# A fused transformer kernel on one core: position bias of the first attention as narrow tile matmuls, one spread matmul issued earlier, and matmuls added beside a bitwise search

## The chip, the cores and the metric

The kernel is one program for one core of a Trainium2 chip. The metric is the device time of one execution in microseconds (us), lower is better. The cores' engines are called by their short names: PE is TensorE (PEld its weight loads), DVE VectorE, ACT ScalarE, POOL GpSimd, SP SyncE, which here only issues DMAs.

## The reference

Eight residual layers run over x of 32 batches x 256 tokens x 128 channels. Three of them matter here.

```python
# layer 1: attention, 16 heads of 8 channels, bias by distance
x = x + _L0_attn_ref(_layernorm(x), Wq, bq, Wk, bk, Wv, bv, rel_bias)
#   scores = einsum('bqhd,bkhd->bhqk', q, k) / sqrt(8) + rel_bias[bucket(k - q)]
#   out = softmax(scores) @ v
# layer 4: experts that choose tokens
#   scores = softmax(xt @ Wr);  G, idx = top_k(scores.T, k)   # k = 2048 of 8192 tokens, 8 experts
# layer 5: state space
#   h = exp(dt*A) * h + (dt*u) * B;  y = sum_n h[n] * C[n]    # 16 states, 256 channels
```

The bucket of the bias depends on n = max(q - k, 0) alone: bucket n for n < 16, then up to bucket 31, which is reached at n near 31 and kept from there on. So the bias of a head is one constant (bucket 31) for keys far behind the query, another (bucket 0) for keys after it, and it varies only in a strip of some 31 keys.

## The kernel before

The eight layers run one after the other, each in a block of its own in which every engine has its own instruction stream, in the order of the Python code; semaphores tie the streams together. Nothing reorders the work but that written order.

**First attention** (`attention` with `causal` false, some 630 us). Work is per batch b (32 of them) in a software pipeline of eight slots j, two heads per slot. In a slot TensorE makes for two heads

- `maxima` (L623, L630): the scores with queries on the partitions, for each half t of the queries, 2 matmuls of 256 columns from 96 contraction rows, plus the bias of the strip from `bmax` through a reversing permutation `flip` (256 columns for t = 0, 320 for t = 1). VectorE reduces them to row maxima (L574).
- `scores_near` (L640): the scores again with keys on the partitions, first 128 keys, 2 matmuls of 256 columns from 128 rows. Their bias is not added by TensorE but by VectorE, `add_band` (L524), on the scores in PSUM; ScalarE takes exp of the sum (L413).
- `scores_far` (L652, L659): the other 128 keys, with the bias by three matmuls of 256 columns (`bexp`, the float32 bias in three bf16 parts). ScalarE takes exp (L416).
- every other slot `values` (L671, L675): probabilities times V for four heads, whose outputs stand on 32 partitions each, so each matmul uses 32 columns of the array at one of four positions. `turn` (L682) transposes them.

The constant part of the bias comes through six contraction rows (`CROW`), three for each half of the keys. The tables of the bias are made at the start by `BiasSetup`: a look-up matmul, a copy, a split into three bf16 parts, a store to DRAM, and loads into `bmax`, `bexp` and, by matmuls (L753) and copies (L562), `band`.

**The search** (`choose`): a 30-step bitwise search for the k-th largest score. Each step counts on VectorE (L1616), sums over partitions by a matmul with one column (L1592) and takes a decision on VectorE (L1619 to L1627).

**The state space layer** (`state_space`): for each group of 512 tokens and each state n of 16, POOL makes the input (L2208), ACT exp (L2369), DVE the scan (L2486) and the product with C (L2498, or POOL for the states in `MOVED` = (2, 5)), PE adds the product up (L2613). C reaches DVE through PSUM: `spread_C` (L2581) writes `CC`, one buffer. `front` puts the next group's projections between them.

Of the kernel before, what the change touches and what calls it, by code (L numbers as in the profile page):

```python
# [146 lines left out]
def attention(nc, res, name, w, causal, held):  # L147
# [5 lines left out]
    BAND = 160  # L153
    FIRST = 8
    K0Q, K1Q = S, (P if causal else S)
    with ExitStack() as ctx:
# [18 lines left out]
        FROM = S - BAND  # L175
# [18 lines left out]
        else:  # L194
            bmax = sc.sb("bmax", [P, H, BAND], BF16)
            bexp = sc.sb("bexp", [P, NPART, H, BAND], BF16)
            flip = sc.sb("flip", [P, P], BF16)
            band = sc.sb("band", [P, H, BAND])
# [6 lines left out]
                "o_ev ot_mm cseq fin rseq yt_mm yt_ev pr_mm pr_done band_mm band_ev biased bsplit bplaced "  # L205
# [3 lines left out]
        BANDS = [range(h, min(h + 3, H)) for h in range(0, H, 3)]  # L209
# [14 lines left out]
        else:  # L224
            loads = [(wqkv[:], w["wqkv"]), (bqk[:], w["bqk"]), (bv[:], w["bv"]), (flip[:], w["flip"])]
# [3 lines left out]
            bias = BiasSetup(nc, sc, w, bmax, bexp, BAND, [Sx[0], Sx[1], SA[0]], probs)  # L229
# [5 lines left out]
        with nc.Block() as block:  # L235

            @block.sync
            def _(sp):
# [4 lines left out]
                def constants(k, sem):  # L243
                    sp.wait_ge(s["k_cleared"], k + 1)
                    sp.dma_start(Kp[k][MROW:MROW + 2], w["krows"][0:2]).then_inc(sem, 16)
                    sp.dma_start(Kp[k][CROW:CROW + 6], w["krows"][2:8]).then_inc(sem, 16)
                    sp.wait_ge(s["cleared"], k + 1)
                    sp.wait_ge(bias.crows_stored, NPART * 16)
                    sp.dma_start(Qp[k][CROW:CROW + 6], bias.crows).then_inc(sem, 16)

                if causal:
                    for k in range(BUF):
                        sp.dma_start(Qp[k][CROW:CROW + 6], w["zrows"]).then_inc(s["consts"], 16)
# [9 lines left out]
                def step(b, k, a, x_, m, c, p):  # L263
                    if a:
                        kb = (k + 3) % BUF
                        dram = packing[kb % 2]

# [3 lines left out]
                        if causal and b == -1:  # L271
                            sp.wait_ge(s["bsplit"], 5)
                            for i in range(NPART):
# [5 lines left out]
                                     parts[:, 1, 0:2, :]).then_inc(s["written"], 16)  # L279
                        wait(sp, s["written"], 32 * (b + 4))  # L280
# [8 lines left out]
                    if not causal and b == -3:  # L289
                        bias.store(sp)  # L290
                        constants(0, s["consts"])
                        constants(1, s["consts"])
# [65 lines left out]
            def _(act):  # L358
# [48 lines left out]
                def step(b, k, a, x_, m, c, p):  # L407
                    for j in range(8):
                        if c:
                            at = 2 * j % NP  # L410
                            wait(act, s["pv_done"], 16 * b + 2 * j + 2 - NP)
                            wait(act, s["sa_mm"] if causal else s["biased"], 8 * b + j + 1)
                            nc.scalar.activation(probs[:, at:at + 2, 0:K0Q], pair(SA[j % 2], K0Q), ACT.Exp)\  # L413
                                .then_inc(s["ea_done"], 1)
                            wait(act, s["sb_mm"], 8 * b + j + 1)
# [22 lines left out]
                    if not causal and b == -2:  # L438
# [3 lines left out]
                        bias.place(act)  # L442
# [4 lines left out]
            def _(v):  # L447
# [2331 lines left out]
```

## Time and profile before

| | |
|---|---|
| median of 3 runs | 3942.99 us (3940.44 to 3944.78) |
| the profiled execution: own time, span | 3959.12 us, 3956.8 us |
| busy share of the span | PE 86%, DVE 73%, ACT 48%, POOL 39% |
| first attention | from about 44 us to 696 us |
| the search | 1514 to 1573 us |
| state space layer | about 2060 to 3040 us |

A share over the whole span mixes layers with different limits, so each layer is read for itself. A matmul's record shows its latency, not the time for which it holds the array: that is read from the distance between the starts of successive matmuls. A float32 matmul leaves two records.

### The profile page before, as it was taken

The numbers are of one execution on the slowest core, as the hardware profiler recorded it, in microseconds if no ns is written. First come the engines' busy times: TensorE is split into PE (matmuls) and PEld (weight loads), VectorE is DVE, ScalarE is ACT, GpSimd is POOL, SyncE is SP. The second block draws the span as 40 slices with busy tenths as digits, with TensorE's granted clock in tenths as the row PEclk, the third lists the DMA queues.
The fourth block names the chain that finished last, engine by engine and source line by source line (L and its number), as shares of the span: only waits on it lengthen the run. The fifth ranks groups of instructions, "written<-read, shape, count | busy, mean of one in ns | idle before, by whom it ended". The sixth has DMA issues, their size and how long they took to land. (4 is left out here: it accounts for less than half of the span.)

```text
span 3956.8 us, 60602 instructions
## 1 busy us (share of the span) xinstructions
PE 3403.3 (86%) x20989; PEld 2093.9 (53%) x21044; DVE 2900.9 (73%) x6458; ACT 1902.9 (48%) x3463; POOL 1549.3 (39%) x1015
## 2 busy tenths in 40 slices
PE   5999999878999984677748888888886999999987
PEld 3677776555777762344423333333333666666653
DVE  7888888556777756433239999999997777777765
ACT  2555556324665651222237676776673333333325
POOL 2311111542211200588848877878873011111112
PEclk9999999999999996799869999999998999999998
DMA  6333332004444424233332332322321222222211
GB/s 154 94 89 90 88 89 54 1 5 115 100 101 104 98 62 122 57 44 44 43 78 73 95 100 83 93 78 73 95 79 60 90 87 87 87 87 87 88 59 43
DMA packets 242530, 314.19 MB, mean 79 GB/s; under 512 B 46450, under 2 KB 157779, under 8 KB 231588
## 3 DMA queue, kind: packets, MB, share of 16 engines
q1 hardware_dynamic: 208308, 289.02, 26.3%
q0 software_dynamic: 22528, 17.32, 3.3%
q10 hardware_dynamic: 11392, 3.97, 0.5%
q8 instruction: 172, 2.82, 0.3%
q14 instruction: 130, 1.06, 0.1%
HBM read 251.93 MB, written 57.08 MB: 78 GB/s over the span
## 5 line engine op out<-in xcount | busy, mean ns | idle before, releaser
L574 DVE TENSOR_REDUCE a_Mx<-a_Sx 128x2 f32<-128x512 f32 (+1 forms) x1024 | 590.3, 618 | 172.2 <-PE a_Sx L626 126.7
L2208 POOL TENSOR_TENSOR a_inp<-a_dtu,a_Bs 128x1024 f32<-128x1024 f32 x256 | 597.8, 2359 | 67.9 <-DMA a_Bs<-a_brows 42.5
L2486 DVE TENSOR_TENSOR_SCAN a_h<-a_dA,a_inp 128x1024 f32<-128x1024 f32 x256 | 583.0, 2283 | 31.7 <-ACT a_dA L2369 27.2
L2613 PE MATMUL a_Y<-a_hc,g_ident 128*128 128x512 f32 x1024 | 487.8, 599 | 7.4 <-POOL a_hc L2222 3.5
L347 POOL TENSOR_TENSOR a_rest<-a_qk,a_parts 128x512 f32<-128x512 f32 x64 | 75.2, 1175 | 916.1 <-ACT a_parts L399 916.1
L413 ACT ACTIVATE a_Pr<-a_SA 128x512 f32<-128x512 f32 x512 | 305.4, 596 | 168.6 <-DVE a_SA L524 79.6
L623 PE MATMUL a_Sx<-att_Kp,att_Qp 96*128 96x256 bf16 (+1 forms) x2048 | 345.3, 261 | 42.7 <-DMA att_Qp<-a_crows 17.9
L2369 ACT ACTIVATE a_dA<-a_dtA,a_A 128x512 f32<-128x512 f32 x512 | 329.8, 681 | 97.5 <-DVE a_h L2486 96.5
L1958 ACT ACTIVATE f_sg<-f_GB 128x512 f32<-128x512 f32 x272 | 162.6, 598 | 436.6 <-PE f_GB L2034 436.4
L2084 PEld LDWEIGHTS f_OUT<-g_routed_wd,f_hm 128*128 128x128 f32 x2176 | 280.6, 191 | 123.5 <-issue 90.5
L2613 PEld LDWEIGHTS a_Y<-a_hc,g_ident 128*128 128x128 f32 x1024 | 195.4, 194 | 234.2 <-issue 223.0
L2498 DVE TENSOR_TENSOR a_hc<-a_h,a_CC 128x1024 f32<-128x1024 f32 x224 | 273.5, 1221 | 43.0 <-DMA f3e_xg<-f_rows,f3e_idx 14.4
L1900 DVE TENSOR_TENSOR f_sg<-f_sg,f_UB 128x512 f32<-128x512 f32 x256 | 175.4, 685 | 168.6 <-PE f_UB L2036 114.7
L2084 PE MATMUL f_OUT<-g_routed_wd,f_hm 128*128 128x128 f32 x2176 | 289.6, 276 | 3.0 <-DVE f_hm L1904 1.4
L416 ACT ACTIVATE a_Pr<-a_SB 128x512 f32<-128x512 f32 (+1 forms) x512 | 253.1, 494 | 60.2 <-PE a_SB L659 37.0
L2034 PE MATMUL f_GB<-f_xnT,g_routed_wg 128*128 128x512 f32 x544 | 280.8, 598 | 0.0
L2036 PE MATMUL f_UB<-f_xnT,g_routed_wu 128*128 128x512 f32 x544 | 278.7, 594 | 0.0
L623 PEld LDWEIGHTS a_Sx<-att_Kp,att_Qp 96*128 96x128 bf16 x2048 | 189.7, 99 | 80.0 <-DVE a_Mx L574 25.8
L1284 POOL DMA_INDIRECT f_sum<-f3e_Y,f3e_idx x128 | 202.7, 1584 | 56.3 <-issue 41.8
L1273 POOL DMA_INDIRECT f3e_xg<-f_rows,f3e_idx x128 | 124.8, 975 | 224.3 <-DVE f3e_idx L1343 185.6
L1904 DVE TENSOR_TENSOR f_hm<-f_sg,f_Cs 128x512 f32<-128x512 f32 x256 | 189.9, 742 | 10.4 <-DMA f_Cs<-f_crows 1.7
L640 PE MATMUL a_SA<-att_Qp,att_Kp 128*128 128x256 bf16 x1024 | 190.2, 274 | 3.0 <-ACT a_Pr L413 0.6
(480 smaller groups left out, 6771.3 us busy)
## 6 DMA issues: line engine op xcount, KB each, us to landing
a_Bs<-a_brows SPq DMA_DIRECT2D x256, 256.0 KB, 3.3
f_Cs<-f_crows SPq DMA_DIRECT2D x512, 128.0 KB, 2.9
att_Qp<-a_packing SPq DMA_DIRECT2D x192, 192.0 KB
att_Kp<-a_packing SPq DMA_DIRECT2D x192, 192.0 KB
a_packing<-a_parts SPq DMA_DIRECT2D x64, 384.0 KB
a_packing<-a_parts SPq DMA_DIRECT2D x64, 128.0 KB
a_Cs<-a_brows SPq DMA_DIRECT2D x32, 256.0 KB, 4.7
g_x<-x SPq DMA_DIRECT2D x8, 512.0 KB, 7.3
```

The costliest lines, as they stand in the source:

```text
L413: nc.scalar.activation(probs[:, at:at + 2, 0:K0Q], pair(SA[j % 2], K0Q), ACT.Exp)\
L416: nc.scalar.activation(probs[:, at:at + 2, K0Q:K0Q + K1Q], pair(SB, K1Q), ACT.Exp)\
L574: nc.vector.tensor_reduce(Mx[(k + 2 - (j < LATE)) % 2][:, t, 2 * jj:2 * jj + 2], Sx[t][:, 0:2 * wd].rearrange("p (h q) -> p h q", h=2), AX ...
L623: nc.tensor.matmul(both[:, u], Qp[kb][0:KM, h, t * P:t * P + P], Kp[kb][0:KM, h, 0:wd], start=(u == 0), stop=False)
L2034: nc.tensor.matmul(GB[k][:], wg[:, q], xnT[j][:], start=True, stop=True).then_inc(s["g_mm"], 1)
L2036: nc.tensor.matmul(UB[k][:], wu[:, q], xnT[j][:], start=True, stop=True).then_inc(s["u_mm"], 1)
L2084: last = nc.tensor.matmul(OUT[j][:, t], hm[k][:, t * P:t * P + P], wd[:, q], start=False, stop=(q == NQ - 1 and t == G - 1))
L2208: nc.gpsimd.tensor_tensor(inp[n % Q][:], dtu[k][:], Bs[n % Q][:].unsqueeze(1).to_broadcast([P, CH, GT]), ALU.mult).then_inc(s["mulB"], 1)
L2369: nc.scalar.activation(dA[m % 2][:, c], dtA[k][:, c], ACT.Exp, scale=A[:, c, n:n + 1])\
L2486: nc.vector.tensor_tensor_scan(h[n % 2][:].rearrange("p c q -> p (c q)"), dA[m % 2][:].rearrange("p c q -> p (c q)"), inp[n % Q][:].rearra ...
L2498: nc.vector.tensor_tensor(hc[n % Q][:], h[n % 2][:], CC[:].unsqueeze(1).to_broadcast([P, CH, GT]), ALU.mult).then_inc(s["mulC"], 1)
L2613: nc.tensor.matmul(Y[c][:], ident[:], hc[n % Q][:, c], start=False, stop=(n == N - 1))\
```

## The change

Three edits. In the first attention the constant part of the bias becomes a step per 32 keys: 24 contraction rows (8 steps x 3 bf16 parts) in place of 6, and the rest, which is not zero only near the diagonal, is added by blocks of 32 rows x 64 columns. One block matmul has 96 contraction rows (the three parts stacked) and 32 outputs, and four of them stand at the four column positions of the array. `maxima`, `scores_near` and `scores_far` each get such a group of four in place of their former bias; `add_band`, `band`, `bmax`, `bexp` and `flip` go. In the state space layer `spread_C` for states 3 and 6 is issued one place earlier, ahead of the sum of states 1 and 4. In the search four matmuls of 512 columns whose result nobody reads follow each one-column matmul.

```diff
@@ maxima
-                            lo, hi = (0, P) if t == 0 else (FROM, S)
-                            last = nc.tensor.matmul(both[:, :, lo:hi], flip[:],
-                                                    bmax[:, 2 * j:2 * j + 2, P * (1 - t) + lo - FROM:P * (1 - t) + hi - FROM],
-                                                    start=False, stop=True)
-                        last.then_inc(s["mx_mm"], 1)
+                            for r in range(4):
+                                q0 = t * P + 32 * r
+                                lo = max(q0 - 32, 0)
+                                last = nc.tensor.matmul(both[32 * r:32 * r + 32, :, lo:q0 + 32], fold[:],
+                                                        near_q[:, 2 * j:2 * j + 2, lo - q0 + 32:64],
+                                                        start=False, stop=True)
+                                last.then_inc(s["mx_mm"], 1)
+                def add_bias(both, h0, first_key, done):
+                    for r in (3, 0, 1, 2):
+                        q0 = first_key + 32 * r
+                        hi = min(q0 + 64, S)
+                        nc.tensor.matmul(both[32 * r:32 * r + 32, :, q0:hi], fold[:], near_k[:, h0:h0 + 2, 0:hi - q0],
+                                         start=False, stop=True).then_inc(done, 1)
@@ scores_near
+                        add_bias(both, h0, 0, s["sa_mm"])
@@ scores_far
-                        for i in range(NPART):
-                            last = nc.tensor.matmul(both[:, :, P:2 * P], flip[:], bexp[:, i, h0:h0 + 2, 0:P],
-                                                    start=False, stop=(i == NPART - 1))
+                        add_bias(both, h0, P, s["sb_mm"])
@@ vector
-                def add_band(b, j):
-                    v.wait_ge(s["sa_mm"], 8 * b + j + 1)
-                    near = pair(SA[j % 2], K0Q)[:, :, 0:BAND]
-                    nc.vector.tensor_tensor(near, near, band[:, 2 * j:2 * j + 2], ALU.add).then_inc(s["biased"], 1)
@@ scalar
-                            wait(act, s["sa_mm"] if causal else s["biased"], 8 * b + j + 1)
+                            wait(act, s["sa_mm"], W * (8 * b + j + 1))
@@ tensor, before the maxima of batch 1
-                            pe.wait_ge(bias.band_placed, NPART * 16)
-                            for g, hs in enumerate(BANDS):
-                                wait(pe, s["band_ev"], g - 1)
-                                for i in range(NPART):
-                                    last = nc.tensor.matmul(
@@ BiasSetup.place, now on the SP queue
-        eng.dma_start(self.bmax[:], bass.AP(self.lines.tensor, N + S - self.BAND,
-                                            [[1, P], [3 * N, H], [1, self.BAND]])).then_inc(self.placed, 16)
-        for i in range(self.NPART):
-            eng.dma_start(self.bexp[:, i], bass.AP(self.lines.tensor, i * H * 3 * N + S - P,
-                                                   [[1, P], [3 * N, H], [1, self.BAND]])).then_inc(self.band_placed, 16)
+        for dst, at, placed in ((self.near_q, 96, self.placed_q), (self.near_k, 0, self.placed_k)):
+            for i in range(self.NPART):
+                eng.dma_start(dst[32 * i:32 * i + 32], bass.AP(self.lines.tensor, i * H * N + at,
+                                                               [[1, 32], [N, H], [1, 64]])).then_inc(placed, 16)
@@ choose, tensor
                 nc.tensor.matmul(CT[:, 0:1], same[:], cnt[:], start=True, stop=True).then_inc(total, 1)
+                for i in range(BESIDE if b < BITS else 0):
+                    nc.tensor.matmul(IDLE[:], identb[:], identb[:].unsqueeze(1).to_broadcast([P, BL, P]),
+                                     start=True, stop=True)
@@ state_space, tensor
-                    if on(0) and n < N - 1 and n + 1 not in MOVED:
+                    if on(0) and n < N - 1 and n not in MOVED and n + 1 not in MOVED:
                         spread_C(g * N + (n + 1), n + 1, k)
@@
                         wait_product(pe, g * N + n)
+                        if n + 1 in MOVED:
+                            spread_C(g * N + (n + 2), n + 2, k)
```

On TensorE a slot of the first attention (one with `values`) reads so before:

```order
L640 MATMUL a_SA<-att_Qp,att_Kp 128x256 x2
L652 MATMUL a_SB<-att_Qp,att_Kp 128x256 x2
L659 MATMUL a_SB<-a_bexp,a_flip 128x2x128 x3
L623 MATMUL a_Sx<-att_Kp,att_Qp 128x256 x2
L630 MATMUL a_Sx<-a_bmax,a_flip 128x2x128
L623 MATMUL a_Sx<-att_Kp,att_Qp 128x256 x2
L630 MATMUL a_Sx<-a_bmax,a_flip 128x2x160
L671 MATMUL a_O<-a_Pr,att_V 32x256 x4
L675 MATMUL a_O<-a_Pr,att_V 32x256 x4
```

And the same slot of the changed kernel:

```order
L635 MATMUL a_SA<-att_Qp,att_Kp 128x256 x2
L627 MATMUL a_SA<-a_near_k,a_fold 32x2x64 x4
L649 MATMUL a_SB<-att_Qp,att_Kp 128x256 x2
L627 MATMUL a_SB<-a_near_k,a_fold 32x2x32
L627 MATMUL a_SB<-a_near_k,a_fold 32x2x64 x3
L606 MATMUL a_Sx<-att_Kp,att_Qp 128x256 x2
L615 MATMUL a_Sx<-a_near_q,a_fold 32x2x32
L615 MATMUL a_Sx<-a_near_q,a_fold 32x2x64 x3
L606 MATMUL a_Sx<-att_Kp,att_Qp 128x256 x2
L615 MATMUL a_Sx<-a_near_q,a_fold 32x2x64 x4
L666 MATMUL a_O<-a_Pr,att_V 32x256 x4
L670 MATMUL a_O<-a_Pr,att_V 32x256 x4
```

Five full-width matmuls are gone (`bexp` three, `bmax` two), and sixteen of 32 outputs have come, in four groups that alternate with pairs of full-width ones; the last group stands directly ahead of `values`.

In the state space layer, TensorE from state 4 to state 7 of a group before (`a_CC` is C of the next state, `a_M` the next group's convolution, `a_Y` the sum over states):

```order
L2557 MATMUL a_M<-a_xnp,g_state_cw 128x512 x2
L2613 MATMUL a_Y<-a_hc,g_ident 128x512 x2
L2581 MATMUL a_CC<-a_bc,g_state_sel 128x512
L2557 MATMUL a_M<-a_xnp,g_state_cw 128x512 x2
L2613 MATMUL a_Y<-a_hc,g_ident 128x512 x2
L2581 MATMUL a_CC<-a_bc,g_state_sel 128x512
```

And of the changed kernel:

```order
L2535 MATMUL a_M<-a_xnp,g_state_cw 128x512 x2
L2559 MATMUL a_CC<-a_bc,g_state_sel 128x512
L2593 MATMUL a_Y<-a_hc,g_ident 128x512 x2
L2535 MATMUL a_M<-a_xnp,g_state_cw 128x512 x2
L2593 MATMUL a_Y<-a_hc,g_ident 128x512 x2
L2559 MATMUL a_CC<-a_bc,g_state_sel 128x512
```

C of state 6 has moved ahead of one sum; C of state 7, the last row, stands where it stood.

On the SP queue, right after the loads of x and the weights, before:

```order
L276 DMA a_packing<-a_parts 128x6x256 [waits a0_split_done,a0_k_cleared,a0_cleared]
L278 DMA a_packing<-a_parts 128x2x256
L285 DMA att_Qp<-a_packing 24x4096 [waits a0_written]
L287 DMA att_Kp<-a_packing 24x4096
...
L825 DMA a_lines<-a_lparts 16x3x1536 [waits a0_bias_seq]
L827 DMA a_crows<-a_lparts 16x2x256 x3
L245 DMA att_Kp<-c_krows 2x4096 [waits a0_k_cleared]
L246 DMA att_Kp<-c_krows 6x4096
L249 DMA att_Qp<-a_crows 6x4096 [waits a0_bias_crows_stored,a0_cleared]
```

And of the changed kernel:

```order
L808 DMA a_lines<-a_lparts 16x3x768 [waits a0_bias_seq]
L275 DMA a_packing<-a_parts 128x6x256 [waits a0_split_done,a0_k_cleared,a0_cleared]
L277 DMA a_packing<-a_parts 128x2x256
L815 DMA a_near_q<-a_lines 32x16x64 [waits a0_bias_stored]
L815 DMA a_near_q<-a_lines 32x16x64 x2
L815 DMA a_near_k<-a_lines 32x16x64 x3
L241 DMA att_Kp<-c_krows 2x4096 [waits a0_k_cleared]
L242 DMA att_Kp<-c_krows 24x4096
L246 DMA att_Qp<-a_lines 8x16x256 [waits a0_bias_stored,a0_cleared]
L246 DMA att_Qp<-a_lines 8x16x256 x2
L287 DMA att_Qp<-a_packing 24x4096 [waits a0_written]
```

The store of the table has moved to the front, and eleven DMAs (six for the blocks, five constants) now stand ahead of the six loads of the first batch's Q and K.

## Rows read from the trace of the kernel before

**Rows 1.** The page: the span.

```profile
span 3956.8 us, 60602 instructions
```

**Rows 2.** Windows of the first attention and the search: busy (count) by engine, PEclk.

```profile
100.00:640.00 540.00, 526.49 (x5157) 378.21 (x5158) 480.86 (x1317) 320.84 (x687) 110.00 (x94) 1.00 0.38 89
1512.00:1574.00 62.00, 18.58 (x65) 15.56 (x63) 45.85 (x213) 0.00 (x0) 0.00 (x0) 0.50 0.37 87
```

**Rows 3.** Timeline of PE in a slot: start, length of the merged records, operation.

```profile
400.15 0.49 PE L659 MATMUL a_SB<-a_bexp,a_flip 128*128 128x256 bf16 x3
400.48 0.38 PE L623 MATMUL a_Sx<-att_Kp,att_Qp 96*128 96x256 bf16 x2
...
402.70 0.30 PE L630 MATMUL a_Sx<-a_bmax,a_flip 128*128 128x320 bf16 x1
402.93 0.64 PE L671 MATMUL a_O<-a_Pr,att_V 128*32 128x256 f32 x8
403.39 0.61 PE L675 MATMUL a_O<-a_Pr,att_V 128*32 128x256 f32 x8
403.94 0.39 PE L640 MATMUL a_SA<-att_Qp,att_Kp 128*128 128x256 bf16 x2
```

**Rows 4.** Weight loads at the same place, with the idle time before them.

```profile
402.93 0.16 PEld L671 LDWEIGHTS a_O<-a_Pr,att_V 128*32 128x32 f32 x8 [0.24 <-issue]
...
403.93 0.11 PEld L640 LDWEIGHTS a_SA<-att_Qp,att_Kp 128*128 128x128 bf16 x2 [0.41 <-issue]
```

**Rows 5.** Groups by line and form over the execution.

```profile
L659 PE MATMUL a_SB<-a_bexp,a_flip 128*128 128x256 bf16 x768 | 125.7, 273 | 0.0
L524 DVE TENSOR_TENSOR a_SA<-a_SA,a_band 128x320 f32<-128x320 f32 x256 | 122.3, 490 | 3.6 <-PE a_SA L640 3.6
```

**Rows 6.** DVE timeline: the same once-a-batch step, 27 batches apart.

```profile
106.69 0.18 DVE L531 TENSOR_SCALAR a_mparts<-a_Mx 128x32 bf16<-128x32 f32 x1
...
638.86 0.18 DVE L531 TENSOR_SCALAR a_mparts<-a_Mx 128x32 bf16<-128x32 f32 x1
```

**Rows 7.** PE timeline in the third layer's attention, around a matmul of 3 rows.

```profile
1003.82 0.49 PE L731 MATMUL a_TURN<-att_wproj,a_yT 128*128 128x128 f32 x2
1004.24 0.23 PE L733 MATMUL a_TURN<-a_bparts,a_onesb 3*128 3x128 bf16 x1
1004.39 0.29 PE L623 MATMUL a_Sx<-att_Kp,att_Qp 96*128 96x128 bf16 x2
```

**Rows 8.** Timeline of the start: first maxima, POOL's wait, band, second maxima.

```profile
44.55 0.61 PE L623 MATMUL a_Sx<-att_Kp,att_Qp 96*128 96x256 bf16 x2 [17.90 <-DMA att_Qp<-a_crows]
...
60.16 1.15 POOL L352 TENSOR_TENSOR a_parts<-a_rest,a_parts 128x512 bf16<-128x512 f32 x1 [1.39 <-DMA att_Kp<-a_packing]
...
65.83 5.37 PE L753 MATMUL a_SA<-a_bexp,a_flip 128*128 128x480 bf16 x18 [8.75 <-DMA a_bexp<-a_lines]
...
71.03 0.38 PE L623 MATMUL a_Sx<-att_Kp,att_Qp 96*128 96x256 bf16 x2
```

**Rows 9.** PE timeline of one search step.

```profile
1535.55 0.58 PE L1592 MATMUL f3c_CT<-f3c_cnt,f_same 128*128 128x1 f32 x2 [1.36 <-DVE f3c_junk L1616]
...
1537.50 0.59 PE L1592 MATMUL f3c_CT<-f3c_cnt,f_same 128*128 128x1 f32 x2 [1.36 <-DVE f3c_junk L1616]
```

**Rows 10.** Line L1022, also one column: nanoseconds min/median/max of a record.

```profile
L1022 PE MATMUL f_SS<-g_ones,f_ssum x128: 250/250/271, 719.1 to 867.4; 128*128 128x1 f32 x128
```

**Rows 11.** State space layer, one group: PE and DVE around states 4 to 7.

```profile
2511.11 1.88 PE L2557 MATMUL a_M<-a_xnp,g_state_cw 128*128 128x512 f32 x4
2512.82 1.88 PE L2613 MATMUL a_Y<-a_hc,g_ident 128*128 128x512 f32 x4
...
2518.19 0.38 PE L2581 MATMUL a_CC<-a_bc,g_state_sel 128*128 128x512 bf16 x1
...
2514.95 1.22 DVE L2498 TENSOR_TENSOR a_hc<-a_h,a_CC 128x1024 f32<-128x1024 f32 x1 [1.05 <-DMA f3e_xg<-f_rows,f3e_idx]
...
2518.61 1.22 DVE L2498 TENSOR_TENSOR a_hc<-a_h,a_CC 128x1024 f32<-128x1024 f32 x1 [0.23 <-PE a_CC L2581]
```

More of the change, by code:

```diff
@@ L194, in attention @@
         else:
[L195 to L198, printed above, removed]
+            near_q, near_k = (sc.sb(n, [NPART * 32, H, 64], BF16) for n in ("near_q", "near_k"))
+            fold = sc.sb("fold", [NPART * 32, 32], BF16)
             tmp, dif, var, nvar = (sc.sb(n, [P, TILES]) for n in ("tmp", "dif", "var", "nvar"))
@@ L228, in attention @@
             x_rows = w["x"].rearrange("b (t p) d -> p (b t) d", p=P)
-            bias = BiasSetup(nc, sc, w, bmax, bexp, BAND, [Sx[0], Sx[1], SA[0]], probs)
+            bias = BiasSetup(nc, sc, w, near_q, near_k, [Sx[0], Sx[1]], probs)
         def pair(bank, wd):
@@ L266, in step @@
                         dram = packing[kb % 2]
+                        if not causal and b == -3:
+                            bias.store(sp)
                         if not causal and b <= 0:
@@ L279, in step @@
                                      parts[:, 1, 0:2, :]).then_inc(s["written"], 16)
+                        if not causal and b == -3:
+                            bias.place(sp)
+                            constants(0, s["consts"])
                         wait(sp, s["written"], 32 * (b + 4))
@@ L639, in scores_near @@
                     for u in range(2):
-                        last = nc.tensor.matmul(both[:, u], K[:, h0 + u, 0:P], Q[:, h0 + u, :],
-                                                start=(u == 0), stop=(u == 1 and not causal))
+                        nc.tensor.matmul(both[:, u], K[:, h0 + u, 0:P], Q[:, h0 + u, :],
+                                                start=(u == 0), stop=False)
                     if causal:
-                        last = nc.tensor.matmul(both[:, :, 0:P], identb[:],
-                                                maskk[:].unsqueeze(1).to_broadcast([P, 2, P]), start=False, stop=True)
-                    last.then_inc(s["sa_mm"], 1)
+                        nc.tensor.matmul(both[:, :, 0:P], identb[:],
+                                         maskk[:].unsqueeze(1).to_broadcast([P, 2, P]), start=False, stop=True)\
+                            .then_inc(s["sa_mm"], 1)
+                    else:
+                        add_bias(both, h0, 0, s["sa_mm"])
                 def scores_far(b, k, j):
@@ L840, in look_up @@
     def look_up(self, pe):
         pe.wait_ge(self.loaded, 32)
-        for i in range(3):
-            self.nc.tensor.matmul(self.LP[i], self.rel[:], self.hot[:, i, :], start=True, stop=True)\
-                .then_inc(self.made, 1)
+        for out, cols in self.LP:
+            self.nc.tensor.matmul(out, self.rel[:], self.hot[:, cols], start=True, stop=True).then_inc(self.made, 1)
     def copy_lines(self, act):
-        N, line = self.N, self.line
-        act.wait_ge(self.made, 3)
-        for i in range(3):
-            self.nc.scalar.activation(line[:, i * N:i * N + N], self.LP[i], ACT.Copy).then_inc(self.got, 1)
+        act.wait_ge(self.made, 2)
```

130 lines of the change are left out of this document (54 added, 76 removed).

## The prediction

> **What bounds the kernel now.** I read the windows first, layer by layer, since a busy share over a span of 3956.8 us [rows 1] mixes eight layers. In the first attention (100 to 640 us) PE is busy for 526.49 of 540 us at full clock, DVE for 480.86, ACT for 320.84 [rows 2]: the layer is TensorE's, with VectorE close behind. The timeline says how full TensorE is. A full-width bf16 matmul of 256 columns holds the array for 0.11 us: three take from 400.15 to 400.48 [rows 3]. So the four of `maxima`, two of `scores_near` and two of `scores_far` take 8 x 0.109 = 0.87 us a slot, and the bias takes 5.25 times 256 columns (256 and 320 in `maxima`, 3 x 256 in `scores_far`), 0.57 us. `values` takes 1.10 us, from the end of L630's columns (402.70 plus 320 columns, 0.134) to L640 at 403.94 [rows 3], four times a batch. With some 3.5 us a batch of transposes and projections that makes 8 x 1.44 + 4.4 + 3.5 = 19.5 us. The batch takes (638.86 - 106.69) / 27 = 19.71 us [rows 6]. Nothing is left over: in the steady part the period is TensorE's instruction stream, and what DVE does there costs nothing.
>
> The second thing to see is what `values` pays. A float32 matmul of 512 columns takes 0.86 us (two take 2511.11 to 2512.82, [rows 11]), so one of 256 takes 0.43, and the eight of `values` would take 3.4 us one after the other. They take 1.10: four of 32 outputs at four column positions run side by side, and two rounds hold the array for 0.86. The remaining 0.24 us stand at the two seams. Columns of the full-width L630 end at 402.83, yet the first tile record and its weight load start at 402.93; and after it PEld sits idle for 0.41 us with no releaser other than issue, until 403.93 [rows 3, 4]. Weight loads, which elsewhere run ahead under the matmul before, don't do so across these seams. The same seam stands between 128 and 3 rows in bf16: L733 starts at 1004.24, its 128 columns are through by 1004.29, and the next full-width matmul starts at 1004.39 [rows 7], 0.10 us later. It is not a matter of float32, then, but of the shape in which the array is divided.
>
> **The change, part by part.**
>
> *Removed on DVE:* 256 `add_band` of 490 ns, 122.3 us [rows 5]. DVE isn't what the period waits for, so I count nothing. It is the term of a rival below.
>
> *Removed on PE:* five bias matmuls a slot, 0.57 us, 4.57 us a batch. The count fits: L659 has 768 records, 3 x 256 [rows 5].
>
> *Added on PE:* four groups of four tiles a slot, each group between full-width matmuls. A group's price g: its columns (128, side by side) 0.053; the seam in 0.10 (402.83 to 402.93) and the seam out 0.10 (1004.29 to 1004.39) make 0.25 us, the low bound. `values`, the only row with four positions, pays 0.24 for both seams with its first weights and the stagger of the four, and the first full-width matmul behind it some 0.01 more: g = 0.24 + 0.01 + 0.05 = 0.30. I take 0.30, since that row has the same four positions and the same 32 outputs, and only the type differs. Per batch 32 groups, 9.6 us. The last group of four slots stands directly ahead of `values` in the same shape, so group and `values` share their seams: 4 x 0.22 = 0.9 us back. Net 9.6 - 0.9 - 4.57 = +4.1 us a batch, on 32 batches +133 us. With g = 0.25: 8.0 - 0.8 - 4.57 = +2.6, +84 us.
>
> The Trainium skill, "TensorEngine Tiling (Array Packing)", section Key Properties, says that a change of tiling mode, other than a change of tile, drains TensorE. The trace agrees, with 0.10 us a seam [rows 3, 7], and by that rule alone the edit has eight drains a slot less the shared ones. A rule that speaks the other way is among the rivals.
>
> *The extra contraction rows* (24 for 6) stand within the 128 rows that `scores_near` and `scores_far` stream anyhow, and `maxima` stays at 96: nothing.
>
> *The start.* Before, PE waits 8.75 us for `bexp` and then makes `band`, from 65.83 to 71.03 [rows 8]. All of that goes. What is late next is batch 1's Q and K, landed by 60.16, when POOL's L352 is let go by them [rows 8]. So the second maxima start some 71.0 - 60.2 = 11 us sooner. Ahead of that the six loads of batch 0 stand behind eleven more DMAs on SP, 0.3 to 0.4 us each to issue, some 4 us; but the first maxima waited for `att_Qp<-a_crows` until 44.55 [rows 8], a wait whose store and loads are now issued earlier, so I set these against each other. -11 us, between -4 (the small block loads crowd the queues) and -17 (the `bexp` traffic gone lets Q and K land sooner).
>
> *The search.* PE runs at half clock there (0.50, [rows 2]). A step takes 1537.50 - 1535.55 = 1.95 us, of which the matmul with one column is 0.58 [rows 9]. The same pair at full clock has records of 250 ns [rows 10], with about 0.11 between their starts, 0.36 in all. The added four take 4 x 0.21 = 0.86 us at full clock and 1.7 at half; they fit into the 1.4 us for which PE idles in a step at the first, and about fill it at the second. If they lift the clock, 0.22 x 28 steps = -6 us; if not, about 0 to +5. I take -5.
>
> *The state space layer.* DVE's product for state 6 waits 1.05 us (the trace names a DMA long done; the wait's other half is C of state 6, which PE writes at about 2514.5, between L2613 and the next L2557), and that of state 7 waits 0.23 [rows 11]. Moved ahead of the sum of state 4, C of state 6 comes 1.7 us sooner and the 1.05 go. But C of state 7 is issued where it was, behind the same work: PE runs without a gap from 2511.11 to 2518.19 [rows 11] and none of it is shorter. DVE then waits 0.23 + 1.05 = 1.28 us for state 7 and goes on at 2518.61 as before. The same holds for state 3. Nothing, and at most 0.2 us a group, -3.
>
> *Sum:* +133 - 11 - 5 = +117 us. On the profiled execution's own 3959.1 that is 4076; the median of the runs, 3943.0, lies 16 below it, so 4060.
>
> **The rivals.**
>
> *A, faster: the seams are hidden.* If the queue pulls the weight loads of bf16 tiles ahead, a group costs its columns and a stagger of 0.02: 0.075 us. The slot then changes by 0.30 - 0.57 = -0.27, the layer by -69 us, and the kernel comes to 3943 - 69 - 16 = 3858. It decides at g = 0.14: below it the layer gains. For it: the groups have no float32, and their weights are the same all the time. Against it: the bf16 seam of [rows 7]. The Trainium skill, "TensorE: Matmul & The Clock Gate", section Part 3: Packing small matmuls, gives for tiles side by side the duration of one plus about 4 ns for each further one, and no price for a change of shape; this rival is what the edit does by that rule. 10 in 100.
>
> *B, slower still: bf16 tiles don't run side by side.* With one after the other a group is 0.25 + 4 x 0.053 = 0.46, the layer 14.7 - 0.9 - 4.57 = +9.2 a batch, +297 us, the kernel 4224. Against it: `values` [rows 3]. 5 in 100.
>
> *C, the relief of DVE counts.* ACT's exp waited for `add_band`; were the loop of PE, DVE and ACT the bound instead of PE's stream, up to 0.49 us a slot would come back, and the seams would be paid out of waits: 4060 - 125 = 3935, about no change. Against it: 19.5 of 19.71 us are PE's own. 5 in 100.
>
> **How the numbers follow.** 80 in 100 for the forecast: 4060. Its bounds: g = 0.25 with the best start and search, 3943 + 84 - 17 - 6 = 4004; g = 0.30 with the worst, 3943 + 133 - 4 + 5 = 4077. Prices that no row has (a weight load of 32 columns under bf16, up to 0.02 us more a tile, half of it exposed: 0.04 x 1024 = +41) open it to 4118, and a little less on a seam to 3990. Range 3990 to 4120. A measurement of this kernel tells about 0.2% from no change; A falls below that, C about on it, B above. Faster 0.13, same 0.03, slower 0.84.
>
> **What would show it.** Right: starts of successive full-width matmuls on both sides of a group of four 0.36 to 0.41 us apart instead of 0.11 without one (a group 0.25 to 0.30); PEld idle "issue" ahead of each group and behind it; a batch of 23.3 to 23.9 us; DVE busy some 3 tenths less in the layer; no L753; second maxima near 60 us; search steps of 1.73 us at clock 1.0; in the state space layer a wait of 1.28 us ahead of state 7's product and none at state 6's, with groups as long as before. Wrong: a period under 19.7 us (seams hidden), tile starts 0.05 us apart (serial), or a state space layer that is shorter by over 3 us.

## The result, and the profile after

The changed kernel takes 4018.63 us (median of 4, 4016.24 to 4021.01) where the one before takes 3943.31 on the same chip: ratio 1.0192, 95% interval 1.0174 to 1.0210, 75.3 us slower. The forecast was 4060 (3990 to 4120), slower.

First the page: the span, then busy time by engine, share of the span and instructions.

```profile
span 4018.8 us, 66208 instructions
...
PE 3514.1 (87%) x23905; PEld 2002.5 (50%) x23960; DVE 2805.9 (70%) x6196; ACT 1919.6 (48%) x3462; POOL 1547.7 (39%) x1015
```

The spans differ by 62.0 us [rows 1], not by 75, because the profiled execution of before took 3959.12 us, 16 over its median, and some 12 of these stand in the experts' stage behind the search, where nothing was changed: the difference between the traces is 74 us at the search's end and 62 behind that stage. Windows of the first attention and of the search:

```profile
100.00:640.00 540.00, 536.60 (x6689) 262.60 (x6688) 358.71 (x968) 295.94 (x607) 96.17 (x82) 1.00 0.34 80
1592.00:1652.00 60.00, 41.37 (x189) 18.11 (x187) 48.32 (x222) 0.00 (x0) 0.00 (x0) 0.93 0.37 85
```

Against [rows 2], DVE falls from 480.86 to 358.71 us and PE rises from 526.49 to 536.60: hardly a gap is left in it. The search runs at 0.93 instead of 0.50. DVE's once-a-batch step gives the period, as [rows 6] did:

```profile
110.30 0.18 DVE L525 TENSOR_SCALAR a_mparts<-a_Mx 128x32 bf16<-128x32 f32 x1
...
711.54 0.18 DVE L525 TENSOR_SCALAR a_mparts<-a_Mx 128x32 bf16<-128x32 f32 x1
```

(711.54 - 110.30) / 27 = 22.27 us a batch, 2.56 more than before; 4.1 were forecast. One of the 27, behind 168 us, holds a wait of 0.85 us for the normalised x and takes 23.15; the others take 22.24. Every kernel below with groups of tiles, except e9, has such a batch, longer by 0.7 us (e5) to 5.1 us (e12), so for these kernels the steady batch is given too. The PE timeline of a slot, which answers to [rows 3], and under it the weight loads, as [rows 4]:

```profile
401.34 0.24 PE L615 MATMUL a_Sx<-a_near_q,a_fold 96*32 96x128 bf16 x4
401.40 0.61 PE L666 MATMUL a_O<-a_Pr,att_V 128*32 128x256 f32 x8
...
402.37 0.39 PE L635 MATMUL a_SA<-att_Qp,att_Kp 128*128 128x256 bf16 x2
402.70 0.24 PE L627 MATMUL a_SA<-a_near_k,a_fold 96*32 96x128 bf16 x4
402.87 0.39 PE L649 MATMUL a_SB<-att_Qp,att_Kp 128*128 128x256 bf16 x2
403.19 0.24 PE L627 MATMUL a_SB<-a_near_k,a_fold 96*32 96x64 bf16 x4
```

```profile
402.69 0.10 PEld L627 LDWEIGHTS a_SA<-a_near_k,a_fold 96*32 96x32 bf16 x4 [0.21 <-issue]
402.87 0.11 PEld L649 LDWEIGHTS a_SB<-att_Qp,att_Kp 128*128 128x128 bf16 x2
...
```

Two full-width matmuls hold the array for 0.22 us, yet L649 starts 0.50 us behind L635: the group of four costs 0.28. L635 has 402.37 + 0.22 = 402.59 as the end of its columns and the first tile starts at 402.70, with PEld idle for "issue" ahead of it; that is the seam in. The group directly ahead of `values`, in the same shape, takes 0.06 (401.34 to 401.40). Groups of the first 800 us, which answer to [rows 5] (busy us, mean ns of one, idle time before and its releaser), first the tiles of `maxima` on PE, then the reductions on DVE:

```profile
L615 PE MATMUL a_Sx<-a_near_q,a_fold 96*32 96x128 bf16 (+1 forms) x2048 | 124.2, 229 | 0.0
```

```profile
L557 DVE TENSOR_REDUCE a_Mx<-a_Sx 128x2 f32<-128x512 f32 x512 | 330.9, 686 | 219.8 <-PE a_Sx L615 214.6
```

DVE's reductions wait 214.6 us for the tiles of `maxima`: in the steady part TensorE alone sets the time. The start, as [rows 8], from the timelines of POOL and PE:

```profile
42.25 1.15 POOL L352 TENSOR_TENSOR a_parts<-a_rest,a_parts 128x512 bf16<-128x512 f32 x1 [12.10 <-DMA att_Kp<-a_packing]
```

```profile
45.25 0.61 PE L606 MATMUL a_Sx<-att_Kp,att_Qp 96*128 96x256 bf16 x2 [19.04 <-DMA att_Qp<-a_lines]
45.79 0.30 PE L615 MATMUL a_Sx<-a_near_q,a_fold 96*32 96x64 bf16 x4
...
61.89 0.58 PE L606 MATMUL a_Sx<-att_Kp,att_Qp 96*128 96x256 bf16 x2
...
86.57 0.39 PE L606 MATMUL a_Sx<-att_Kp,att_Qp 96*128 96x256 bf16 x2
86.89 0.24 PE L615 MATMUL a_Sx<-a_near_q,a_fold 96*32 96x128 bf16 x4
```

The second maxima start at 61.89, 9.1 us sooner than before, yet batch 1's maxima end 1.2 us later. The reason is TensorE's pace: at 45.25 the tiles start 0.54 us behind the pair, at 86.57 it is 0.32. The pair's own starts are 0.19 apart until 86 us and 0.12 from there on. Before, the pace is the slow one until 48.4 us and again, while TensorE mostly waits, from 58.9 to 69.2 us (the last section has the clock). The search and the state space layer, as [rows 9] and [rows 11]:

```profile
1612.12 0.38 PE L1567 MATMUL f3c_CT<-f3c_cnt,f_same 128*128 128x1 f32 x2 [0.48 <-DVE f3c_junk L1594]
1612.36 1.02 PE L1569 MATMUL f3c_IDLE<-g_identb 128*128 128x512 bf16 x4
1613.87 0.38 PE L1567 MATMUL f3c_CT<-f3c_cnt,f_same 128*128 128x1 f32 x2 [0.48 <-DVE f3c_junk L1594]
```

```profile
2635.31 1.22 DVE L2476 TENSOR_TENSOR a_hc<-a_h,a_CC 128x1024 f32<-128x1024 f32 x1
...
2639.92 1.22 DVE L2476 TENSOR_TENSOR a_hc<-a_h,a_CC 128x1024 f32<-128x1024 f32 x1 [1.19 <-PE a_CC L2559]
```

A search step takes 1.75 us. In the state space layer state 6's product waits no more and state 7's waits 1.19.

### The profile page after: what moved, and what is told of

It reads as the page before. It is cut to its first block and busy times, and to the rows that moved or that the text cites. A ratio compares the mean times of both kernels' runs of the same rounds, so it can differ in the third digit from the quotient of the medians.

```text
span 4018.8 us, 66208 instructions
## 1 busy us (share of the span) xinstructions
PE 3514.1 (87%) x23905; PEld 2002.5 (50%) x23960; DVE 2805.9 (70%) x6196; ACT 1919.6 (48%) x3462; POOL 1547.7 (39%) x1015
## 5 line engine op out<-in xcount | busy, mean ns | idle before, releaser
L557 DVE TENSOR_REDUCE a_Mx<-a_Sx 128x2 f32<-128x512 f32 (+1 forms) x1024 | 592.3, 619 | 348.5 <-PE a_Sx L615 214.6
L606 PE MATMUL a_Sx<-att_Kp,att_Qp 96*128 96x256 bf16 (+1 forms) x2048 | 367.6, 267 | 42.0 <-DMA att_Qp<-a_lines 19.0
L405 ACT ACTIVATE a_osb<-a_O 128x256 f32<-128x256 f32 x256 | 98.1, 383 | 245.3 <-PE a_O L670 245.3
L606 PEld LDWEIGHTS a_Sx<-att_Kp,att_Qp 96*128 96x128 bf16 x2048 | 153.2, 98 | 96.1 <-DVE a_Mx L557 20.0
L635 PE MATMUL a_SA<-att_Qp,att_Kp 128*128 128x256 bf16 x1024 | 197.1, 276 | 0.4 <-ACT a_Pr L413 0.2
```

What stands on the lines that cost most here:

```text
L557: nc.vector.tensor_reduce(Mx[(k + 2 - (j < LATE)) % 2][:, t, 2 * jj:2 * jj + 2], Sx[t][:, 0:2 * wd].rearrange("p (h q) -> p h q", h=2), AX ...
L606: nc.tensor.matmul(both[:, u], Qp[kb][0:KM, h, t * P:t * P + P], Kp[kb][0:KM, h, 0:wd], start=(u == 0), stop=False)
```

## The experiments

**Theory:** a group of tiles costs its two seams with full-width work, and the rest of the loss against the forecast is TensorE time that before was waiting and not work. **Rivals:** the price is in the tiles themselves; the other two edits, or the relief of DVE, matter. Batch lengths are made like the 22.27 above. Chips differ: before took 3943 to 3958 us in the four sets, so a time is read as its ratio to before of its own set, and 1.0192 is the changed kernel's.

**The parts alone.** e1 is the changed kernel without the edits of the search and the state space layer.

```diff
-                    nc.tensor.matmul(IDLE[:], identb[:], ...)        # and the two edits of spread_C undone
```

> Only the attention edit stands; the search and the state space layer are as before. Theory (changes of the array's shape carry the loss): 4018.6 plus the 5.7 us that the search had gained in the trace, about 4024, +81 us on before (4020 to 4028). Rival (the busy TensorE in the search or the moved broadcasts cost time elsewhere that hides a dearer or a cheaper attention): under 4010 or over 4035.

Measured: 4037.86 to 3955.67 us (before), ratio 1.0207 (1.0193 to 1.0221), +82 us. The attention carries the whole loss.

```diff
+                for i in range(BESIDE if b < BITS else 0):
+                    nc.tensor.matmul(IDLE[:], identb[:], ...)        # e2: before, with this alone
```

> Kernel before with only the four idle matmuls beside each step of the search. Theory: they keep the granted clock up, a step takes 1.77 instead of 1.96 us, -5.7 us in all, -0.14%. Rival (the gain in the trace came from the run, or the four stand in the way of the wait for the count): 0 or up to +5 us, with the clock of the stretch at 0.5.

Measured: 3939.45 to 3943.45, ratio 0.9986 (0.9977 to 0.9995), -4 to -6 us, as forecast.

```diff
-                    if on(0) and n < N - 1 and n + 1 not in MOVED:
+                    if on(0) and n < N - 1 and n not in MOVED and n + 1 not in MOVED:
                         spread_C(g * N + (n + 1), n + 1, k)
...
+                        if n + 1 in MOVED:                               # e3: before, with this alone
+                            spread_C(g * N + (n + 2), n + 2, k)
```

> Kernel before with only the earlier broadcast of C for states 3 and 6. Theory (the wait is handed on to states 4 and 7, whose C stays behind the same sums): 0, within 3 us, groups of 59.2 us as before. Rival (the earlier product frees something else): -3 to -16 us.

Measured: 3942.36 to 3943.45, ratio 0.9998 (0.9989 to 1.0007): nothing. The wait had only moved to state 7.

e8 adds to e3, in the same place, C of states 4 and 7, which leave their old one:

```diff
+                        if n in MOVED:
+                            spread_C(g * N + (n + 2), n + 2, k)
```

> As the run with the spread alone, and C of states 4 and 7 too is issued ahead of the sum of the state before the last, that of 2 and 5. Theory (states 4 and 7 were where the wait went, 1.19 us ahead of state 7's product and 0.2 ahead of state 4's): VectorE gets 1.1 to 1.4 us a group back, 16 groups, -18 to -22 us on before. Rival 1 (TensorE stalls on the wait for state 6's product, or the wait is handed on again): 0 to -5 us. Rival 2 (partly handed on to a scan that waits for ScalarE's decay): -5 to -15.

Measured: 3943.88 to 3943.45, ratio 1.0000 (0.9991 to 1.0009). The time is rival 1's, the mechanism the one that rival 2 named. DVE's timeline of e8 says where the wait went:

```profile
2563.40 1.22 DVE L2498 TENSOR_TENSOR a_hc<-a_h,a_CC 128x1024 f32<-128x1024 f32 x1
2566.00 2.29 DVE L2486 TENSOR_TENSOR_SCAN a_h<-a_dA,a_inp 128x1024 f32<-128x1024 f32 x1 [1.38 <-ACT a_dA L2369]
```

State 7's product runs at once, and the scan of state 9 now waits 1.38 us for ScalarE's exp (0.34 before). A group of 512 tokens takes 59.2 to 60.3 us in before, e3 and e8 alike. That the chain of `front` and ScalarE sets this length is read from this wait; no run tested it.

**What a group of tiles costs.** e5 keeps all 16 tiles of a slot and halves the seams:

```diff
-                        add_bias(both, h0, 0, s["sa_mm"])      # behind scores_near, and again behind scores_far
+                        groups.append((both, h0, 0, s["sa_mm"]))
...
                             scores_far(b, k, j)
+                            blocks()                           # both groups, 8 tiles
```

and in `maxima` both halves' full-width matmuls come first, then both groups.

> Changed kernel with its 16 tiles a slot unchanged, but in two runs instead of four: the full-width matmuls of scores_near and scores_far, then both groups; those of both maxima, then both groups. Theory (a group's price is its two seams of about 0.10 us, its tiles are cheap): two pairs of seams a slot less, 2 x 0.20 x 8 = 3.2 us a batch, batch 22.27 to about 19.0, kernel 4018.6 - 102 = 3917 (3905 to 3935). Rival 1 (the price is each tile's own weight load and position, 0.07 us a tile): batch stays at 22.3, kernel 4019. Rival 2 (maxima that come later make VectorE and ScalarE the bound): a batch of over 20.5, kernel over 3960, with waits of TensorE for red_done or the exp.

Measured: 3939.99 to 3955.67 us, ratio 0.9958 (0.9944 to 0.9971), faster than before; against the changed kernel that is 1.0192 - 0.9958 = 2.3%, 92 us. 102 us were expected. Batch (628.57 - 107.34) / 27 = 19.30 us, 19.28 steady. PE timeline of e5:

```profile
401.77 0.38 PE L656 MATMUL a_SB<-att_Qp,att_Kp 128*128 128x256 bf16 x2
402.08 0.24 PE L627 MATMUL a_SA<-a_near_k,a_fold 96*32 96x128 bf16 x4
402.15 0.23 PE L627 MATMUL a_SB<-a_near_k,a_fold 96*32 96x64 bf16 x4
402.31 0.61 PE L606 MATMUL a_Sx<-att_Kp,att_Qp 96*128 96x256 bf16 x4
```

The second group costs 0.07 us (402.08 to 402.15). From the end of L656's columns (401.77 + 0.22) to L606 there are 0.32 us; less the two groups' 0.07 + 0.05 of columns, 0.20 are left for one pair of seams. The batch says the same: 2.97 us less for 16 pairs of seams, and one wait back (12.0 us in 28 times, for ScalarE's `mrow`, 0.43 a batch), make 3.4 / 16 = 0.21 us. Every tile also raises a semaphore; e5 keeps all of these, so they are not the price.

e9 does the opposite, eight tiles in each group of the changed kernel and no more seams; the extra four multiply a block of zeros.

```diff
+                        nc.tensor.matmul(both[32 * r:32 * r + 32, :, q0:hi], nothing[:], near_k[:, h0:h0 + 2, 0:hi - q0],
+                                         start=False, stop=False)
```

> Changed kernel with eight tiles in each group instead of four: the first four multiply a block of zeros into the same places, so the output stays the reference's, and no change of the array's shape is added. Theory (a further tile set costs its 0.053 us of columns and some 0.013 of stagger, the seams are the rest of a group's 0.28): 32 x 0.066 = 2.1 us a batch, batch 24.4, kernel 1.019 of before plus 68, about 4087 where before takes 3943 (4070 to 4105). Rival (the price is in the tiles, their weight loads and positions, not in the seams): 32 x 0.28 = 8.9 us a batch, kernel about 4300.

Measured: 4087.26 to 3958.15, ratio 1.0326 (1.0310 to 1.0342), 53 us over 1.0192 where the theory said 68. Batch (760.84 - 114.63) / 27 = 23.93 us, 1.69 more than the steady 22.24 for 32 sets: 0.053 us each, the columns alone. So of 0.28 us a group is 0.05 of work and about 0.22 of seams. The rival of dear tiles is out.

The Trainium skill, "TensorEngine Tiling (Array Packing)", section Key Properties, has the drain at a change of mode, without a price; here it is 0.21 us a pair. "TensorE: Matmul & The Clock Gate", section Part 3: Packing small matmuls, has one duration plus some 4 ns for each further tile. With the columns' 0.053 us for that duration, an estimate by its figure is 0.053 + 3 x 0.004 = 0.065 us for a group; the 0.07 of e5 agrees, and the four tiles of a group start 3 or 4 ns apart in the traces.

e6 goes on: all 16 tiles of a slot in one run.

```diff
-                            blocks()                           # behind scores_far
...
+                        blocks()                               # behind the full-width matmuls of maxima
```

> As the run with pairs, but all 16 tiles of a slot in one run behind the six full-width groups, so one pair of seams a slot. Theory of the seams: three pairs less than in the changed kernel, 3 x 0.20 x 8 = 4.8 us a batch, batch 17.5, kernel 4018.6 - 150 = 3869 (3850 to 3895), faster than before. Rival 1 (tiles' own price): 4019. Rival 2 (the loop of TensorE, VectorE and ScalarE binds once the groups come so late): the gain over the run with pairs is under a third of the theory's 1.6 us a batch, and TensorE shows waits for it.

Measured: 3956.72 to 3955.67, ratio 1.0001 (0.9992 to 1.0010), batch (643.12 - 105.81) / 27 = 19.90 us, 19.73 steady; 3869 us had been expected. The seams went (PE is busy for 452.03 of 500 us, 487.18 in e5), and waits took their place. The view of waits of e6, 106 to 620 us (total, times, longest):

```profile
PE a_TURN L760 <- ACT a_mrow L422: 31.4, 26, 1.2
PE a_Sx L606 <- DVE a_Mx L557: 5.7, 28, 0.2
PE a_SB L657 <- ACT a_Pr L416: 4.1, 25, 0.2
```

That is rival 2. The likely reason, not tested apart: results come in one burst at the slot's end, ScalarE and VectorE have nothing to do until then, and TensorE waits for them in the next slot. e11 takes e6 and puts `scores_far` behind the full-width matmuls of `maxima`, which it does in the third layer's attention too.

```diff
                             if j < 7:
                                 scores_near(b, k, j + 1)
-                            scores_far(b, k, j)
...
+                    if between:                                # in maxima, ahead of blocks()
+                        between()                              # scores_far(b, k, j)
```

> As the run with all groups in one, with the full-width matmuls of scores_far behind those of the maxima instead of ahead of them. Theory (that run's 19.9 us a batch hold 18.0 of work; its waits are TensorE's for the exp of the one far bank and for the reductions of the two maxima banks): the far bank's wait goes, that of the maxima banks, which now come 0.22 us sooner behind the groups, grows; batch 18.8 to 19.8, 3910 to 3950 where before takes 3943. Rival 1 (the far bank's exp was what bound it): batch 18.2 to 18.8, 3890 to 3910, faster than the run with pairs. Rival 2 (the loop over VectorE's reductions binds alone): batch 19.9 or more.

Measured: 4019.86 to 3958.15, ratio 1.0150 (1.0136 to 1.0164), far outside the 3910 to 3950 expected. Its first layer's batch is (678.79 - 109.27) / 27 = 21.09 us, 21.02 steady; some 25 us more were lost in the third layer. Waits of e11, 109 to 620 us:

```profile
PE a_TURN L764 <- ACT a_mrow L422: 29.0, 24, 1.2
PE a_Sx L606 <- DVE a_Mx L557: 22.5, 75, 0.5
```

The far bank's wait is gone and that for the reductions went from 5.7 to 22.5 us, as rival 2 had it (the loop through the two maxima banks). But the wait for `mrow`, the longest in both, stayed, and which of the two binds no run separates.

**What DVE's addition cost.** e4 is the kernel before without `add_band`; its near scores lack their bias.

```diff
-                            wait(act, s["sa_mm"] if causal else s["biased"], 8 * b + j + 1)
+                            wait(act, s["sa_mm"], 8 * b + j + 1)
-                            if j == 0:
-                                add_band(b, 0)
-                            if j < 7:
-                                add_band(b, j + 1)
```

> Kernel before, with add_band left out (the scores' near keys then lack their bias; maxima and far scores keep theirs), so that the exp of the near scores waits for TensorE alone, 3.9 us of VectorE a batch less. Theory (some 1 us of a batch's 19.71 was waiting in TensorE's stream for ScalarE and VectorE, which the edit removes beside the matmuls): batch 18.8 to 19.2, kernel 3943 - 16 to - 29, 3914 to 3927. Rival (as predicted: the stream alone is the period, relief is worth nothing): 3943, within 4 us.

Measured: 3940.33 to 3955.67, ratio 0.9967 (0.9955 to 0.9979), 13 us, a little less than the 16 to 29 of the theory but clear of the rival's 4. Batch (624.75 - 106.62) / 27 = 19.19 us, 0.52 less. The same place of a batch in the PE timeline, first before, then e4:

```profile
413.53 0.44 PE L776 MATMUL a_TURN<-g_ident,a_xn 128*128 128x128 f32 x2
414.04 0.39 PE L640 MATMUL a_SA<-att_Qp,att_Kp 128*128 128x256 bf16 x2
414.53 0.39 PE L652 MATMUL a_SB<-att_Qp,att_Kp 128*128 128x256 bf16 x2
```

```profile
405.67 0.44 PE L771 MATMUL a_TURN<-g_ident,a_xn 128*128 128x128 f32 x2
405.94 0.38 PE L635 MATMUL a_SA<-att_Qp,att_Kp 128*128 128x256 bf16 x2
406.16 0.38 PE L647 MATMUL a_SB<-att_Qp,att_Kp 128*128 128x256 bf16 x2
```

From L776 to L652 there are 1.00 us before and 0.49 in e4: 0.51 us a batch in which L640 and L652 wait for the exp behind `add_band`. The profile names no wait there, since a record's length covers it; only the distance between starts shows it.

e7 puts such an addition, of zeros, back into the changed kernel, ahead of each near exp, and the exp waits for it again.

```diff
+                    near = pair(SA[j % 2], K0Q)[:, :, 0:160]
+                    nc.vector.tensor_tensor(near, near, zeros[:], ALU.add).then_inc(s["biased"], 1)
```

> Changed kernel with an addition of zeros of the old size (128x320 float32 in the bank of the near scores) put back on VectorE ahead of every near exp; the output stays the reference's. Theory (the changed kernel's stream waits 0.28 us a batch for others where the one before waited 1.0, because this addition is gone): +0.3 to +0.7 us a batch, +10 to +23 us on the changed kernel's 4018.6 of its own chip. Rival (the waits went because the stream got longer, not because VectorE was relieved): within 4 us of the changed kernel.

Measured: 4018.80 to 3943.45, ratio 1.0189 (1.0175 to 1.0203), equal to the changed kernel; batch (714.91 - 111.26) / 27 = 22.36 us, but the 0.09 more come from the one long batch (25.51 us), and the steady batch is 22.24 in both. My theory fell: the waits are gone not because DVE was relieved but because the slot has become long enough for either.

**The start.** e10 is the changed kernel with the packing loads of the first batch ahead of the constants and the block loads, and the constants of the second buffer on a semaphore of their own.

```diff
-                            bias.place(sp)                     # ahead of the packing loads
-                            constants(0, s["consts"])
...
+                        constants(0, s["consts"])              # behind them
+                        bias.place(sp)
-                        constants(1, s["consts"])
+                        constants(1, s["mid_consts"])
```

> Changed kernel with the packing loads of the first batch ahead of the step rows, the constant rows and the block loads on SyncE's queue, and the first maxima waiting for the constants of their own buffer alone, not for those of the second buffer too. Theory (what the start lost against the forecast is Q and K of batch 0 landing at 42.25 instead of 35.66 us, behind transfers of 1.3 MB that are issued ahead of them): first maxima 2 to 3 us sooner than 45.25, kernel 0 to -3 us on the changed one. Rival 1 (the transfers take the same time whatever their order, since the constants are waited for too): 0. Rival 2 (the start lies at the half clock of the tiles and the second batch's Q and K): first maxima sooner, first normalised batch at 62.6 as before, kernel 0.

Measured: 4024.81 to 3958.15, ratio 1.0172 (1.0158 to 1.0186), 0.2% under the changed kernel, with intervals that touch. From the timelines of e10:

```profile
34.85 1.15 POOL L351 TENSOR_TENSOR a_parts<-a_rest,a_parts 128x512 bf16<-128x512 f32 x1 [4.87 <-DMA att_Kp<-a_packing]
```

```profile
39.83 0.58 PE L605 MATMUL a_Sx<-att_Kp,att_Qp 96*128 96x256 bf16 x2 [13.79 <-DMA a_near_q<-a_lines]
```

Q and K land 7.4 us sooner and the first maxima start 5.4 us sooner, more than the 2 to 3 expected; 5.1 of these are left at batch 2 (105.23 against 110.30) and 3.3 at batch 31, since the long batch is longer here. TensorE's slow pace lasts to 80.4 us all the same.

**A faster version.** e12 is e5 with the projection and the addition of V one slot later, in both attentions.

```diff
-                        if a and j == 5:
+                        if a and j == 6:
```

> The run with groups in pairs, with the projection and the addition of V in slot 6 of a batch instead of slot 5, so that they don't wait for mrow, which is made in slot 5. Theory (the one wait that TensorE's stream keeps in that run, 0.5 us a batch ahead of the projection of V, is real and goes): batch 19.30 to 18.8, 32 x 0.5 = -16 us on that run, about 3911 where before takes 3943 (3905 to 3918), the fastest of all. Rival (VectorE, which now adds V behind the reductions of slot 5 and ahead of those of slot 6, hands the wait on): -5 to +5 us on the run with pairs.

Measured: 3932.25 to 3958.15, ratio 0.9932 (0.9918 to 0.9946), the fastest kernel here, 0.7% under before. But the reason is not the one given. In the first layer a steady batch takes 19.30 us (19.28 in e5), though TensorE has no wait for `mrow` left: the rival was right there. The starts show where a part of the wait went: between two pairs of L606, which otherwise start 0.11 us apart, stand 0.31 us twice a batch, in e5 once. The batch of the third layer fell from 17.29 to 16.97 us, which makes the 10 us.

## Why the prediction was right, and where its sizes were off

- **What bounds the layer: right, but not to the last us.** "Nothing is left over" failed. Of 19.71 us, 0.51 were waits behind `add_band` (e4) and 0.33 the wait for `mrow`, which before has 26 times in these 27 batches:

```profile
PE a_TURN L765 <- ACT a_mrow L422: 8.9, 26, 0.4
```

  Own work was 18.9 us, not 19.5. What was too high is the "some 3.5 us a batch of transposes and projections", for which no row was given: by the distances between starts they take 2.6 us (0.87 `turn`, 0.86 and 0.52 the projections, 0.28 and 0.11 the other transposes). The added work was therefore partly laid into waits.
- **The group's price: mechanism right, size a little high.** 0.28 us instead of 0.30; 32 x 0.02 = 0.7 us a batch. With both, 18.9 + 32 x 0.277 - 0.9 - 4.57 = 22.3 us, against 22.24 measured. So the term of +133 us is 32 x 2.56 = +82, which is below its own low bound of +84, and the batch lies below the 23.3 to 23.9 us named as the sign of being right. This is the largest miss of the sum, 51 us.
- **The start: -4 us for -11.** The layer as a whole is 78.2 us longer (batch 31's step 674.79 before, 753.02 after), so what is left over for the start, beside the 82, is -4, the least that the forecast allowed. The wait for `bexp` did go, and the second maxima came at 61.89, near the 60 named. Two things stood against the gain: the new loads put Q and K of batch 0 behind them (e10, 5 us), and TensorE ran at half pace until 86 us, 38 us beyond the first rise of before. What the pace cost no run separates. I had set the DMAs against an earlier store; I had not thought of the pace.
- **The search: right.** 1.75 us a step where 1.73 was named, -5.7 us by the trace, -4 by e2's medians.
- **The state space layer: right.** No wait at state 6, 1.19 us at state 7 where 1.28 was named, and nothing gained. e8 shows that the group was not bound by state 7's wait either.
- **Rivals.** A and B are out (e5, e9). C existed at an eighth of its price: it named up to 0.49 us a slot (3.9 a batch), 0.51 a batch were there.
- Sum: 82 - 4 + 2 (mostly the third layer's first batches, which differ by as much among traces in which nothing was changed there) - 6 = +74 us, against 75.3 measured.
- **Luck in the number.** The median lies 41 us under the 4060 and inside the range only because the low end had been opened for a group of 0.25 us and less. The waits, which took half of the miss in the period, were in no bound. The 0.02 us more a tile for a weight load, which opened the upper end, no run shows: the added tiles of e9 cost their columns alone.

## What to carry to other kernels

Small tiles are nearly free beside each other (0.05 to 0.07 us for four of 128 columns) and dear at their borders with full-width matmuls (0.21 us a pair of borders): count the changes of shape, not the tiles, and batch them, up to the point where waits for the engines behind eat the gain (e6, e11). When an engine seems to be fully its own bound, check the distances between starts for waits that the busy share covers, because added work fills these first. Where a wait is taken from an engine and the period stays, follow it: e3 handed it to the next state, e8 to ScalarE's exp, e12 to other matmuls of the slot.

## What the runs showed of the hardware

- The granted clock ahead of its first record. From 44 to 62 and 62 to 86 us of the changed kernel the windows print PEclk 1.00:

```profile
44.00:62.00 18.00, 16.32 (x107) 6.70 (x108) 11.31 (x20) 1.85 (x4) 1.70 (x2) 1.00 0.69 140
62.00:86.00 24.00, 23.27 (x167) 8.88 (x166) 12.28 (x21) 7.63 (x14) 5.15 (x5) 1.00 0.31 74
```

  That is no reading of the clock: the trace's first clock record starts at 86.3 us, and the windows count a stretch without a record as full. The pace tells more: the two matmuls of a pair start 0.19 us apart until then and 0.12 after. Where a record of the lower level (1.2 GHz) exists, the pace is the same slow one, as in e9, whose pairs of full-width matmuls start 0.19 us apart until 87 us:

```profile
64.20:88.10 23.90, 23.82 (x238) 9.00 (x238) 11.02 (x20) 7.41 (x14) 4.92 (x5) 0.50 0.31 73
88.10:108.00 19.90, 19.90 (x340) 9.71 (x337) 12.13 (x32) 9.13 (x19) 0.00 (x0) 1.00 0.37 90
```

- When it rose. All kernels with groups of tiles come to stay at the full clock only at 80 to 88 us (e6 and e9 have it for 3.4 us near 61 to 66 as well). Before and e4, which have no groups, reach it at 48.7 and 51.6 us, lose it from 58.9 and 61.8 for 10.3 us, and then keep it to the end of the layer. PE had been idle for 19 us ahead of the first maxima in the changed kernel and 18 in before, so it is what PE does afterwards that differs. That the short empty stretches at the seams are the cause is argued, not shown, and one thing speaks against it: the same seams stand in every later slot of the changed kernel, and the clock stays full from 86.3 to 775.8 us. The Trainium skill, "TensorE: Matmul & The Clock Gate", section A second HAM failure mode: psum-queue depth-cycling, tells of a clock that falls and rises again and again when TensorE idles briefly between groups; that is not seen at the seams here. The clock fell once more in e6, e7 and e10 (3.4 us) and in e12, from 160.4 to 167.2 us (a batch of 24.4 instead of 19.3 us), 0.3 to 3 us behind a wait for the normalised x (1.87, 0.83, 0.84 and 1.85 us); the changed kernel and e11 have this wait too (0.85 and 1.38 us) and no fall. The window of e12 and its PE timeline (0.42 us from L642 to L656 is the slow pace, 0.22 the full one):

```profile
160.40:167.20 6.80, 6.80 (x47) 3.93 (x46) 3.38 (x10) 3.46 (x8) 1.30 (x2) 0.50 0.06 12
```

```profile
160.14 0.50 PE L770 MATMUL a_TURN<-g_ident,a_xn 128*128 128x128 f32 x2 [1.85 <-DVE a_xn L535]
160.44 0.63 PE L642 MATMUL a_SA<-att_Qp,att_Kp 128*128 128x256 bf16 x2
160.86 0.64 PE L656 MATMUL a_SB<-att_Qp,att_Kp 128*128 128x256 bf16 x2
```

- Loads in short rows (64 keys, 128 bytes) can hold SyncE's queue: the same three issues of `near_k` on SyncE took 1.55 us in the changed kernel, where they were issued ahead of Q, K and the constants, and 5.83 us in e10, behind them (those of `near_q` 1.94 and 4.29 us). That transfers in flight are the reason is the likely reading, not a tested one.

```profile
23.68 1.55 SPq L815 DMA_DIRECT2D a_near_k<-a_lines  x3
```

```profile
32.41 5.83 SPq L816 DMA_DIRECT2D a_near_k<-a_lines  x3
```
